# Both layer norms' normalization on ScalarE, and the output projection's offset added in the second norm

## The reference, cut to what matters

```python
emb = silu(_sin_emb(timestep)) @ W_ada + b_ada
scale, shift = split(emb)
x = _ln(src) * (1.0 + scale) + shift             # first norm, over the 512 features
q, k, v = x @ Wq + bq, x @ Wk + bk, x @ Wv + bv
probs = softmax(where(src_mask, -inf, q @ k.T / sqrt(32) + attention_bias))   # by head
x = x + (probs @ v @ Wo + bo)                    # bo: the output projection's offset
h = _ln(x) * g2 + beta2                          # second norm
ff = _gelu2(h @ W1 + b1) @ W2 + b2               # _gelu2(a) = a * sigmoid(1.702 * a)
return x + ff                                    # _ln(a) = (a - mean) / sqrt(var + 1e-5)
```

## Time and profile before

| what | us |
|---|---|
| median of 3 runs | 2465.89 (2464.13 to 2466.8) |
| the profiled execution | 2472.93 |
| its span, first to last instruction | 2471.1 |
| TensorE busy | 2363.4 (96%) |
| VectorE busy | 1830.4 (74%) |
| GpSimd busy | 1840.8 (74%) |
| ScalarE busy | 1323.4 (54%) |
| TensorE's mean granted clock | 0.988 of full |

### The profile page before, as it was taken

How to read it: one execution, slowest core, us unless ns; L and a number is a source line. 1 busy time by engine, 2 the same in 40 slices (tenths; PEclk the granted TensorE clock), 3 DMA queues, 4 the chain that set the end, 5 groups by cost and what they waited for, 6 DMA issues and landing times.

```text
span 2471.1 us, 61234 instructions
## 1 busy us (share of the span) xinstructions
PE 2363.4 (96%) x21010; PEld 2234.2 (90%) x21010; DVE 1830.4 (74%) x2921; ACT 1323.4 (54%) x3663; POOL 1840.8 (74%) x1785
## 2 busy tenths in 40 slices
PE   4999999999999999987999999999989999999998
PEld 3888888888888888867999999999979999999998
DVE  4788888888888888777666666666577676777776
ACT  2566666566666666575555555555543333343332
POOL 3777777777777777778777777777896777767675
PEclk8999999999999999999999999999999999999999
DMA  7344444344434444333343434343465556555563
GB/s 241 109 134 134 139 140 134 110 134 139 139 115 137 135 139 136 102 90 122 147 159 136 161 144 154 141 161 146 159 219 170 185 181 188 184 183 187 170 196 125
DMA packets 288978, 372.26 MB, mean 151 GB/s; under 512 B 28544, under 2 KB 202752, under 8 KB 288768
## 3 DMA queue, kind: packets, MB, share of 16 engines
q1 hardware_dynamic: 288768, 369.57, 46.2%
HBM read 251.81 MB, written 117.70 MB: 150 GB/s over the span
## 4 chain that ended last, share of the span: by engine, by line
PE 85%; DVE 5%; issue 3%; POOL 3%; ACT 1%; DMA 1%; SPq 0%; DVEq 0%; POOLq 0%; ACTq 0%
PE up L1568 14%; PE up L1566 14%; PE up L1567 14%; PE turn L923 5%; PE psD L923 4%; PE psD L924 4%; PE psD L925 4%; PE turn L925 4%; PE turn L924 4%; PE psS L952 4%; PE psC L962 2%; PE psS L938 2%; PE turn L1566 2%; PE turn L1567 2%; PE turn L1568 2%
## 5 line engine op out<-in xcount | busy, mean ns | idle before, releaser
L1566 PE MATMUL up<-T,wc 128*128 128x256 f32 x1792 | 511.2, 285 | 14.7 <-DVE gu L1440 7.0
L1568 PE MATMUL up<-T,wc 128*128 128x256 f32 x1792 | 508.0, 283 | 0.0
L1567 PE MATMUL up<-T,wc 128*128 128x256 f32 x1792 | 505.4, 282 | 0.0
L597 POOL TENSOR_TENSOR s<-s,rinv 128x512 f32<-128x512 f32 x254 | 265.2, 1045 | 234.2 <-DVE rinv L791 231.7
L713 ACT ACTIVATE s<-s,nmx 128x128 f32<-128x128 f32 x1024 | 396.2, 394 | 5.5 <-issue 5.5
L1566 PE MATMUL up<-wc,gs 128*128 128x256 f32 x1280 | 360.2, 281 | 3.2 <-DVE gs L1523 3.2
L657 POOL TENSOR_TENSOR bias<-bias,mneg 128x512 f32<-128x512 f32 x256 | 351.8, 1394 | 13.7 <-DVE mneg L796 13.7
L1567 PE MATMUL up<-wc,gs 128*128 128x256 f32 x1280 | 359.9, 281 | 0.0
L1568 PE MATMUL up<-wc,gs 128*128 128x256 f32 x1280 | 359.8, 281 | 0.0
L1566 PEld LDWEIGHTS up<-T,wc 128*128 128x128 f32 x1792 | 339.3, 189 | 18.5 <-DVE gu L1440 8.4
L1567 PEld LDWEIGHTS up<-T,wc 128*128 128x128 f32 x1792 | 340.7, 190 | 0.0
(11 more groups left out here) (209 smaller groups left out, 7043.8 us busy)
## 6 DMA issues: line engine op xcount, KB each, us to landing
bias<-in_bias SPq DMA_DIRECT2D x128, 512.0 KB, 5.4
gated<-gu SPq DMA_DIRECT2D x128, 512.0 KB, 2.6
adab<-ada_rows SPq DMA_DIRECT2D x64, 512.0 KB, 5.5
gbuf<-gated SPq DMA_DIRECT2D x64, 512.0 KB, 3.9
gu<-gated SPq DMA_DIRECT2D x63, 512.0 KB, 3.9
xin<-in_x SPq DMA_DIRECT2D x32, 512.0 KB, 5.1
resid<-rout SPq DMA_DIRECT2D x64, 256.0 KB, 2.2
r<-resid SPq DMA_DIRECT2D x16, 1024.0 KB, 6.0
```

Source lines behind the costliest of these rows:

```text
L597: eng.tensor_tensor(s[:, b, heads, :], s[:, b, heads, :], rinv[:, b, heads].unsqueeze(2).to_broadcast([P, HG, S]), ALU.mult).then_inc(done, 1)
L1566: pe.matmul(out_ap, sh, mh, start=start, stop=False)
L1567: pe.matmul(out_ap, sh, ml, start=False, stop=False)
L1568: return pe.matmul(out_ap, sl, mh, start=False, stop=stop)
```

## The change

- First norm: DVE makes only `offset = -mean * rstd` (128x2), and ACT makes `xn = rstd * xin + offset`, one operation of 512 for each batch, in front of the high part of the turned rows.
- Second norm: the same with `offset2` (128x4). Beside groups 1 to 13 the four ACT operations stand together after the second gate of unit 7, ahead of the next group's `p1c`; for the rows of group 1 they stand in unit 1 of group 0, for group 2 at the end of its unit 7, for group 0 in the last steps of attention.
- `bo` is no longer added in attention; `resid` is stored without it, and `add_bo` adds it to the four rows of `r` read back: three additions behind `c11` of unit 4 and one behind `c11` of unit 5, the `spread` moved behind `c11` of unit 6; for group 0 in the step `end == -7` of attention, for group 1 in the last step, for group 2 in units 6 and 7. The down stage's `b2` gets `bo` added once.
- The end of DVE's attention loop moves behind the maxima of the second batch of a pair; the statistics move into `second_half`.
- In group 0 the second turn stands in unit 5 instead of 4.
- In the last group one factor's sums move from POOL to DVE (`sums_early`), the first two gate sums too (`early_two`), and the sums of factor J+4 from before the down stage to its unit 0.

```diff
-    def normalize(self, dve, q, u, b):
+    def center(self, dve, q):
         at_least(dve, self.rstd_ready, q + 1)
-        at_least(dve, self.res_half, q * 2 + (b - 1))
-        dve.tensor_scalar(self.xn[:, b, :], self.xin[:, u, b, :], self.mean[:, b:b + 1], self.rstd[:, b:b + 1],
-                          ALU.subtract, ALU.mult).then_inc(self.xn_ready, 1)
+        dve.scalar_tensor_tensor(out=self.offset[:, :], in0=self.mean[:, :], scalar=-1.0, in1=self.rstd[:, :],
+                                 op0=ALU.mult, op1=ALU.mult).then_inc(self.offset_ready, 1)
+
+    def normalize(self, act, q, u, b):
+        at_least(act, self.offset_ready, q + 1)
+        at_least(act, self.res_half, q * 2 + (b - 1))
+        act.activation(self.xn[:, b, :], self.xin[:, u, b, :], ACT.Identity, scale=self.rstd[:, b:b + 1],
+                       bias=self.offset[:, b:b + 1]).then_inc(self.xn_ready, 1)
...
+    def add_bo(self, dve, n, b):
+        at_least(dve, self.r_in, (n + 1) * DMA)
+        dve.tensor_tensor(self.of(n)[:, b, :], self.of(n)[:, b, :], self.bo[...], ALU.add).then_inc(self.bo_added, 1)
...
                 if on.proj:
                     copy(*kq, 3)
+                if on.norm:
+                    if b:
+                        norm.normalize(act, p + 3, (u + 3) % 2, 0)
+                    else:
+                        norm.normalize(act, p + 2, u % 2, 1)
                 if on.turn:
                     norm.high(act, p + 2, u % 2, b)
...
                 dve.tensor_tensor(rout[:, b, :], psD[0][:, :], norm.xres[:, slot, b, :], ALU.add).then_inc(r_ready, 1)
-                at_least(dve, r_ready, t + 1)
-                dve.tensor_tensor(rout[:, b, :], rout[:, b, :], bo_bc[:, :], ALU.add).then_inc(bo_added, 1)
...
                 if on.end == -7:
                     for m in range(second.NB):
+                        second.add_bo(dve, 0, m)
+                    for m in range(second.NB):
                         second.statistics(dve, 0, m)
...
+                second_half(first, first % UNROLL, 0, steady(0))
+                first_half(first, first % UNROLL, 1, steady(1))
                 with dve.Fori(0, (last - first + 1) // UNROLL) as i:
-                    for m in range(2 * UNROLL):
+                    for m in range(1, 2 * UNROLL + 1):
...
         def turns_at(first):
-            return (2, 4) if first else (0, 2)
+            return (2, 5) if first else (0, 2)
...
-            return {1: 0, 2: 1, 4: 2, 5: 3}.get(j)
+            return {1: 0, 4: 2, 5: 3}.get(j)
...
-                if fixed(n) and n == LAST and j >= 6:
-                    sums(j - 6, j - 6)
...
             def before_down():
                 c22_u4(K - 1, 3)
-                weights.sums(pool, J + 4)
-                sums(2, 2)
                 gather(K - 2, 2)
                 gather(K - 1, 3)
+                sums(2, 2)
...
+                if first and j == 1:
+                    for b in range(NB):
+                        norm.normalize(act, n + 1, b)
+                if has(n, 2) and j == 7 and not first:
+                    for b in range(NB):
+                        norm.normalize(act, n + 2, b)
...
                 c11(k, j % 4)
+                if not first and has(n, 2):
+                    if j == 4:
+                        for b in range(3):
+                            norm.add_bo(dve, n + 2, b)
+                    if j == 5:
+                        norm.add_bo(dve, n + 2, 3)
+                    if j == 6:
+                        norm.spread(dve, n + 2)
+                    if j == 7:
+                        norm.center(dve, n + 2)
```

More of the change, by code:

```diff
@@ L440, in _ @@
             act.activation(expm[:, :], emb[:, :], ACT.Exp, scale=-1.0).then_inc(exp_ok, 1)
+            norm.normalize(act, 0, 0, 0)
             for i in range(3):
@@ L641, in step @@
                 if on.end == 0:
+                    sp.wait_ge(v_done, B)
+                    sp.dma_start(second.bo[1], d["bo"].rearrange("(a f) -> a f", a=1).to_broadcast([P, DM])).then_inc(second.bo_in, DMA)
                     for m in (2, 3):
@@ L750, in step @@
                     exps(t, b, 2)
+                if on.end in (-6, -5):
+                    for m in range(2):
+                        second.normalize(act, 0, (on.end + 6) * 2 + m)
                 if on.split_o:
@@ L831, in first_half @@
                     for m in range(second.NB):
-                        second.statistics(dve, 1, m)
+                        second.add_bo(dve, 1, m)
                 else:
@@ L881, in second_half @@
                     for m in range(second.NB):
+                        second.add_bo(dve, 0, m)
+                    for m in range(second.NB):
                         second.statistics(dve, 0, m)
                     second.spread(dve, 0)
-                if on.end in (-6, -5):
-                    for m in range(2):
-                        second.normalize(dve, 0, (on.end + 6) * 2 + m)
+                if on.end == -6:
+                    second.center(dve, 0)
                 if on.end == 0:
@@ L890, in second_half @@
                         weights.low(dve, 0, piece)
+                if on.end == 1:
+                    for m in range(second.NB):
+                        second.statistics(dve, 1, m)
                 if on.split_o:
@@ L1312, in down @@
                         finish(n - 1, 1 - u, m)
-                if first and j in (0, 1, 3):
-                    weights.sums(pool, J + (5, 6, None, 7)[j])
-                if first and j == 2:
-                    pool.wait_ge(b2_in, DMA)
+                if first and j < 4:
+                    weights.sums(pool, J + 4 + j)
+                if first and j == 4:
+                    pool.wait_ge(b2_in, 2 * DMA)
+                    pool.tensor_tensor(bb[:, :], bb[:, :], c1.rearrange("p i n -> p (i n)"), ALU.add).then_inc(bb_sum, 1)
+                    pool.wait_ge(bb_sum, 1)
                     pool.tensor_tensor(bb[:, H:], bb[:, H:], bb[:, 0:H], ALU.subtract).then_inc(bb_ready, 1)
@@ L1383, in up @@
                                 norm.high(act, n + 1, 1 - u, e, piece)
+                if first and j == 7:
+                    for b in range(NB):
+                        norm.normalize(act, n + 2, b)
             def before_down():
@@ L1476, in late @@
                     if first and j in (6, 7):
-                        norm.statistics(dve, n + 2, 2 * (j - 6))
-                        norm.statistics(dve, n + 2, 2 * (j - 6) + 1)
+                        dve.wait_ge(norm.bo_in, DMA)
+                        for b in range(2):
+                            norm.add_bo(dve, n + 2, 2 * (j - 6) + b)
+                        for b in range(2):
+                            norm.statistics(dve, n + 2, 2 * (j - 6) + b)
                     if not first and j in (5, 6):
                         norm.statistics(dve, n + 2, j - 3)
-                    if j == (7 if first else 6):
+                    if first and j == 7:
                         norm.spread(dve, n + 2)
-                    if not first and j == 7:
-                        norm.normalize(dve, n + 2, 0)
-                        norm.normalize(dve, n + 2, 1)
                 if fixed(n) and n == LAST and j == 7:
@@ L1500, in up @@
                 if first and j == 1:
-                    for b in range(NB):
-                        norm.normalize(dve, n + 1, b)
+                    norm.center(dve, n + 1)
                 if first and j + 2 < J:
```

77 lines of the change are left out of this document (49 added, 28 removed).

## The result

The changed kernel takes 2500.3 us (median of 4 runs, 2488.1 to 2515.7) against 2466.35 for the kernel before in the same session: 1.0131 times, 95% interval 1.0107 to 1.0155. It is slower by 34 us. The forecast was 2469.9 with a range to 2484, so the result lies 30 us above the forecast and 16 above the range. The profiled execution took 2498.74 us (span 2496.9), 25.8 more than that of before.

What follows compares the result with a forecast made beforehand. TensorE, 85% of the chain, bounds the kernel, so only its idle time can be won. Terms -14.7 + 0.3 + 3.3 + 18.3 + 1.3 - 4.5 = +4.0 on 2465.9 give 2469.9 us, range 2451 to 2484.

Steps and rivals of the forecast that it cites:

- Up loop: 13 groups of the up stage: TensorE stalls 1.41 us a group at product 5, waiting for p1c; +18.3 us.
- a: Up loop, VectorE: sum of a group's four bo additions, taken as 3.9 us, between 2.44 and 5.3.
- a - 2.49: Up loop: TensorE's stall per group in us, with a floor of 0.15; 1.41 at the a taken.
- Rival C: Up loop: additions pay in full and more, a = 5.3, stall 2.81, +36.5; total 2490.6 us; chance 0.13.
- First norm on ScalarE: Attention: one ScalarE operation per batch, about 0.81 us alone; nothing in steady attention, +0.3 us at the startup.
- Loop end: Attention: branch behind the second batch's maxima, its idle time falls into an existing wait; -14.7 us.
- Additions for group 0: Attention: four bo additions, all on the path where TensorE already waits; +3.3 us (2.4 to 4.6).
- First up group: Group 0 of the up stage: 4.8 us of waits won, 6.1 added; net +1.3 us (-4 to +6).
- Transition: Up to down stage: GpSimd loses sums ahead of the last factor TensorE waits for; -4.5 us (-2 to -14.4).
- D: Attention: the late reciprocal delays the probabilities, half of the 14.7 stays, +7.4; total 2477.3 us; chance 0.08.
- E: Transition: all 14.4 us of TensorE's idle time goes, -9.9 more; total 2460.0 us; chance 0.09.
- B: Additions hidden, GpSimd pays: a is 2.6, stall 0.15 a group (+2.0); total 2451.7 us; chance 0.27.

Runs made afterwards that it cites:

- f4: Changed kernel with offset and offset2 put into unused bytes of other tensors' slots, so all other tensors lie at their old addresses; 2516.22 us, 1.0181.
- g1: f4 with the addition of bo back in attention and none in the second norm, normalizations still on ScalarE; 2492.5 us, 1.0105.
- e4: Changed kernel with the four ScalarE normalizations moved from ahead of the next group's p1c to right behind it; 2466.2 us, 1.0017.
- e1: Changed kernel with spread's wait for the normalization (xn_ready) moved from VectorE to GpSimd's rstd; 2483.79 us, 1.0081.
- g3: Kernel before with only VectorE's loop end moved behind the second batch's maxima, statistics and spread into second_half; 2448.24 us, 0.9925.
- g4: g2 and g3 together on the kernel before: wc aligned and loop end moved; 2415.26 us, 0.9782.
- g2: Kernel before with 32 unused bytes ahead of wc and 32 ahead of gu, putting wc at 95296; 2435.62 us, 0.9894.
- h3: Kernel before with 60 one-element memsets on VectorE right ahead of its attention loop; 2476.14 us in its one run.
- h2: g4 with the transition's edits of the change (sums moved between GpSimd and VectorE, and later); 2436.94 us.
- f1: Kernel before with only the two new tensors declared, unused, which moves wc from byte 95264 to 95296; 2440.34 us, 0.9923.

## Why the prediction was wrong

Measured against f4, which has the change at the addresses of before, step by step:

*Up loop, forecast +18.3, measured +37.2.* This is the step that failed by most, and by size, not by mechanism. VectorE in the changed kernel, units 4 to 7 of a steady group:

```profile
1300.06 0.42 DVE L1487 TENSOR_TENSOR gu<-up,p1c 128x256 f32<-128x256 f32 x1 [0.99 <-PE up L1637]
1300.40 3.07 DVE L219 TENSOR_TENSOR r<-r,b_bc 128x512 f32<-128x512 f32 x3
1303.39 0.41 DVE L1492 TENSOR_TENSOR gu<-up,gu 128x256 f32<-128x256 f32 x1
...
1307.02 1.23 DVE L219 TENSOR_TENSOR r<-r,b_bc 128x512 f32<-128x512 f32 x1
1308.17 0.41 DVE L1492 TENSOR_TENSOR gu<-up,gu 128x256 f32<-128x256 f32 x1
...
1316.78 0.41 DVE L1487 TENSOR_TENSOR gu<-up,p1c 128x256 f32<-128x256 f32 x1
1317.11 0.59 DVE L239 SCALAR_TENSOR_TENSOR offset<-mean,rstd 128x4 f32<-128x4 f32 x1
```

Three additions from 1300.40 to 1303.39 and one from 1307.02 to 1308.17: a = 4.14, where I took 3.9. The offset, 128x4, takes 0.6 and not 0.20 (from 0.13 to 0.69 in its 16 rows); it too has two inputs from SBUF and stands beside a busy GpSimd, which is the likely reason but not shown by a run of its own. I had priced it by its size. ScalarE and TensorE behind it:

```profile
1315.96 0.71 ACT L1393 ACTIVATE gu<-gu,b_c 128x512 f32<-128x512 f32 x1
1317.74 2.93 ACT L244 ACTIVATE r<-r,offset,rstd 128x512 f32<-128x512 f32 x4 [1.07 <-DVE offset L239]
1320.58 0.36 ACT L1378 ACTIVATE p1c<-up 128x256 f32<-128x256 f32 x1
```

```profile
1320.99 0.38 PE L1635 MATMUL up<-T,wc 128*128 128x256 f32 x1 [2.50 <-ACT p1c L1378]
```

The four in a row start 0.71 apart (1317.74 to 1320.58 is 2.84), as worked out. From c11 to product 5 it takes 4.21 (1316.78 to 1320.99) instead of the 3.75 forecast, 0.46 more, nearly all of it the offset's. The formula a - 2.49 gives 1.65, with this 0.46 it is 2.11; f4 shows 29.2/13 = 2.25. In the changed kernel the unit is 4.95 long instead of 5.04, so that product 5 comes earlier by three units' 0.09, and the wait is 2.50. That makes 13 x 2.25 = 29 us of the 37. The other part I had priced at nothing: the granted clock. TensorE stands still for over 2 us at each start of a group and runs in some groups at the lower of its two levels (1.2 GHz) for a while. Two groups of f4, with a wait of 2.2 and of 2.5 us at their start, the first at full clock and the second not (columns as in the earlier trace rows):

```profile
1361.00:1405.00 44.00, 42.31 (x352) 42.10 (x352) 29.97 (x62) 25.24 (x48) 33.54 (x41) 1.00 0.38 143
1633.00:1677.00 44.00, 42.36 (x342) 42.15 (x340) 28.49 (x58) 24.39 (x46) 33.55 (x41) 0.96 0.35 130
```

From one p1c of unit 0 to the next, the first of them lasts 44.5 us and the second 46.0. In all, the lower level holds for 17 us of f4's loop and 20 of the changed kernel's, which costs 8.5 and 10 us; the kernel before has none of it. 29 and 8.5 make up the 37. g1 with its 1.25 us waits and e4 with 0.5 us waits have no such stretch from group 2 on.

That such an addition and a GpSimd operation hold each other up was the Trainium skill's rule ("SBUF — State Buffer", "Who interferes with whom"), and the trace agrees: the additions start 1.0 us apart instead of 0.61, while GpSimd's operations in the same stretch got longer too, against the 0.74 of the earlier trace rows:

```profile
1300.58 1.19 POOL L1291 TENSOR_TENSOR gu<-gu,p5c 128x256 f32<-128x256 f32 x1
1301.73 1.18 POOL L1298 TENSOR_TENSOR s1p<-gu 128x256 f32<-128x256 f32 x1
```

Both engines pay. What I drew from the rule was wrong in one point: that the normalizations that go away, with one such input, had been cheap beside GpSimd. In the trace of before, the first norm's took 0.53 us in its shortest row and 1.57 in the median:

```profile
L120 DVE TENSOR_SCALAR xn<-xin,mean,rstd x64: 530/1566/1580, 16.4 to 1014.2; 128x512 f32<-128x512 f32 x64
```

GpSimd was at work beside 62 of these 64. No term of the sum hung on it, since the two that the up loop loses were priced by their rows.

Rival C's price, 36.5, is what came, but by luck and not by its way: a is 4.14 and not 5.3. The sign that I had given for C, additions above 1.2 in the rows of their line, did appear (median 1.23 of 56), but such a row overlaps the next operation, and in a row they start 1.0 apart: the sign was badly chosen.

*First norm on ScalarE, forecast nothing in steady attention.* Failed outright. I followed xn to those who read it and to the turned rows behind it on ScalarE, and not to who waits for it to be over: `spread` on VectorE begins with a wait for xn_ready, since it overwrites what the normalization read. While both were on VectorE this cost nothing. Now VectorE stands there in every second batch (95.7 us in 21 waits), the residual comes late, and a pair of batches takes 32.32 us instead of 31.68, some 0.18 of it by xT's address. Over 24 pairs that is 11 us, and e1, which takes all waits away, has attention 12.4 us shorter. The operation's own length came as estimated, 0.80 us for 0.81.

*Loop end, forecast -14.7.* TensorE's waits were of this size and are all gone (g3), but a loop's end cost more than these waits: g4's 52 batches are 19.8 us shorter than g2's, and the medians fell by 22 (g3) and 20 (g4 against g2). What the other 5 us are is open. The way was nearly right: I let the 5.1 us stay and hoped to hide them in VectorE's wait for psC. They are covered by the operations queued when the sequencer takes the branch, and h3 shows that it isn't the position in the instruction stream by 60 instructions. In the changed kernel the gain is eaten by the step above: f4 is 3.2 us later at the fifth context split (forecast 0.3), takes 5.6 less for the next 52 batches and 3.0 more for the rest, +0.6 for all of attention.

*Additions for group 0, forecast +3.3.* The wait for `v` rose from 2.0 to 5.2, +3.2:

```profile
PE turn L965 <- DVE v L812: 5.2, 1, 5.2
```

*First up group, forecast +1.3, measured +9.0.* TensorE's waits there sum up to 20.3 us in f4 instead of 17.1 in the earlier trace rows's view, with a new one of 4.0 for T. The rest is clock: the mean from 1105 on is 0.86 over 80 us in f4 against 0.93 over 71, which is 6 us. Again the clock, and again not priced.

*Transition, forecast -4.5, measured 0.* GpSimd's sums of J+5 to J+7 take 6.2 us each in f4 where two of them took 4.6 and 5.3, beside VectorE, and GpSimd has new waits of 2.1 and 1.8. h2 confirms it: nothing.

*What no step had.* Two tensors of 8 and 16 bytes a partition move wc by 32, and the matmuls' pitch with it. That is -28 us in f1, and it is why the changed kernel is 1.3% slower and not 1.8%.

So the mechanism of the up loop was forecast and under-priced (the offset, the clock), while the first norm's path was missed. Of the rivals, D (the loop's end keeps half of its stall) and E (the transition gives all) are refuted, B (additions hidden) too. The forecast's chances had slower as the likeliest of the three, at 0.38, of which 0.17 was the upper end of its own range and 0.21 rivals C and D, not the reasons that came; the range ended at 2484, 16 us short.

## What to carry to other kernels

When an operation moves to another engine, list not only who reads what it writes but every wait on its semaphore, also the ones that guard an overwriting: those were free while both stood on one engine. Operations put ahead of a copy that frees a PSUM bank are paid by TensorE as soon as what they wait for is late: 1.25 us a group without the additions (g1), 2.25 with them, and there in some groups in clock too. The same four behind the copy cost over a third of that. Hide a pause behind a loop's branch with work queued ahead of the branch. And compare kernels at equal addresses: a small new tensor in front of a large matmul operand was worth more here than most of the edits.

## What the runs showed of the hardware that was not expected

- The pitch of 128x256 fp32r matmuls with no wait around them depends on where wc lies in SBUF: 0.120 us at a multiple of 128 bytes, 0.1173 or 0.1187 at 32 past it, 0.1133 or 0.1178 at 64 past it (moving operand wc in the down stage, full clock in all of them).
- With wc at 64 past, the down stage's pitch takes one of two levels (0.1133 and 0.1178 in traces), and the runs of one kernel on one chip fall into two heaps at the distance that this gives: f1's ten are six of 2438 to 2440 and four of 2462 to 2463. What chooses is open. At a multiple of 128 there was one level only (ten runs within 5 us).
- A VectorE operation on 128x4 with two SBUF inputs (the offset) took 0.59 instead of 0.16 to 0.2 beside a busy GpSimd, and the normalization with one SBUF tensor and two 128x1 operands (L120) 1.57 in the median instead of 0.53.
- Behind the branch that closes attention's loop VectorE was idle for 4.1 to 5.1 us where it had next to nothing queued, for 1.4 us in e1 with 1.7 us queued, and not at all with 3.6 us queued (g3). Leaving the loop cost nothing (next operation 0.2 us behind the branch). Shifting the loop by 60 instructions changed nothing. What the sequencer does in the pause is open.
